# First layer: the adjacency loaded by converting transfers behind x, the first queries computed among the values, the mask stored later, and the queries' halves copied on SyncE's queue

## The reference

```python
h = relu(layernorm(x))
q, k, v = heads(h @ Wq.T + bq), heads(h @ Wk.T + bk), heads(h @ Wv.T + bv)    # 4 heads of 64
kc, vc = k and v cut into 8 chunks of 256 nodes
scores = clip(q @ kc.T / 8, -10, 10)                 # for each chunk
scores = where(mask == 0, -10, scores)               # mask = adj
ctx = sum over chunks of softmax(scores within the chunk) @ vc
out = layernorm(ctx @ Wo.T + bo + h) * gamma + beta
x = x + out
# second layer: additive attention over all 2048 nodes, masked by adj, softmax, elu; then x = x + that
```

## Time and profile before

| | us |
|---|---|
| median of 3 runs | 4921.1 |
| lowest, highest | 4913.72, 4924.88 |
| the profiled execution: time | 4913.24 |
| the profiled execution: span of the trace | 4911.4 |
| busy: PE, DVE, ACT, POOL | 4741.8, 3719.8, 2978.2, 1423.7 |
| first score product of batch 0 starts at | 105.11 |
| second layer's first instructions at | 3438.18 |

### The profile page before, as it was taken

One profiled execution on the slowest core, in us unless ns is written; L12 is line 12 of the kernel. 1 busy time (PEld: TensorE's weight loads), 2 busy tenths in 40 slices (PEclk: granted clock), 3 DMA queues, 4 the chain that ended last, 5 costly groups with the idle time before them and its releaser, 6 DMA issues. The chain is left out here.

```text
span 4911.4 us, 135734 instructions
## 1 busy us (share of the span) xinstructions
PE 4741.8 (97%) x56349; PEld 4357.3 (89%) x56349; DVE 3719.8 (76%) x7056; ACT 2978.2 (61%) x3317; POOL 1423.7 (29%) x1685
## 2 busy tenths in 40 slices
PE   6999999999999999999999999998899999999999
PEld 4998899898899988989988998987799999999998
DVE  6676666676676766666676676666899999999999
ACT  4444444444444444444444444443899999999998
POOL 3344334344334434434433443333100100000000
PEclk9999999999999999999999999999899999999999
DMA  6000100001000001001001000010421221221221
GB/s 214 18 18 18 30 19 27 23 18 27 19 23 27 18 23 27 18 19 31 18 18 32 18 27 18 17 40 12 114 73 36 76 74 35 76 78 31 76 65 37
DMA packets 173923, 195.25 MB, mean 40 GB/s; under 512 B 7520, under 2 KB 157408, under 8 KB 171104
## 3 DMA queue, kind: packets, MB, share of 16 engines
q1 hardware_dynamic: 158256, 142.70, 9.7%
q0 software_dynamic: 15024, 43.53, 3.6%
HBM read 110.43 MB, written 38.03 MB: 30 GB/s over the span
## 5 line engine op out<-in xcount | busy, mean ns | idle before, releaser
L797 ACT ACTIVATE slot<-slot,shift 128x1024 f32<-128x1024 f32 x1024 | 1113.6, 1088 | 1588.1 <-PE slot L651 1588.1
L661 PEld LDWEIGHTS outs<-v_s,probs 128*128 128x128 f32 x16384 | 1980.9, 192 | 103.5 <-issue 25.4
L661 PE MATMUL outs<-v_s,probs 128*128 128x128 f32 x16384 | 1991.6, 275 | 0.0
L941 DVE SCALAR_TENSOR_TENSOR probs<-slot,bound 128x1024 f32<-128x1024 f32 x1024 | 1253.2, 1224 | 681.2 <-ACT slot L797 678.3
L1577 ACT ACTIVATE u<-s_all,d_sign 128x1024 bf16<-128x1024 f32 x1024 | 1117.6, 1139 | 58.0 <-PE sums L1478 38.6
L459 POOL TENSOR_TENSOR ctx_sum<-ctx_sum,ctx_part 128x256 f32<-128x256 f32 x896 | 651.2, 732 | 1043.0 <-DVE ctx_part L957 1042.6
L650 PE MATMUL slot<-q_hl,k_hl 128*128 128x512 f32 x2048 | 897.4, 438 | 28.4 <-DVE probs L941 11.4
L651 PE MATMUL slot<-q_hl,k_hl 128*128 128x512 f32 x2048 | 805.0, 393 | 0.0
L1474 PE MATMUL sums<-x_mixed,u 128*128 128x130 f16 x8192 | 786.1, 219 | 2.0 <-issue 1.9
L1478 PE MATMUL sums<-x_mixed,mask 128*128 128x65 f16 x8192 | 759.5, 194 | 5.5 <-issue 5.5
L1709 DVE TENSOR_TENSOR u<-u,mask 128x1024 f16<-128x1024 bf16 x1024 | 688.1, 682 | 77.7 <-ACT u L1577 69.6
(11 more groups left out here) (161 smaller groups left out, 3766.6 us busy)
## 6 DMA issues: line engine op xcount, KB each, us to landing
q_hl<-q_hl POOLq DMA_DIRECT2D x128, 256.0 KB, 3.6
s_all<-s_turned SPq DMA_DIRECT2D x64, 512.0 KB, 5.5
x_q_s<-in_x SPq DMA_DIRECT2D x32, 512.0 KB, 4.8
x<-y SPq DMA_DIRECT2D x32, 512.0 KB, 3.2
t_o_s<-x SPq DMA_DIRECT2D x16, 1024.0 KB, 6.0
out<-t_o_s SPq DMA_DIRECT2D x16, 1024.0 KB, 6.8
x_q_s<-x SPq DMA_DIRECT2D x28, 512.0 KB, 6.1
probs<-in_adj SPq DMA_DIRECT2D x11, 1024.0 KB, 5.6
```

Source lines behind the costliest of these rows:

```text
L661: end = nc.tensor.matmul(outs[i % OUTS][:, q, :], probs[:, i % PROBS, r, q * P:(q + 1) * P], v_s[:, c * JC + r, h * E1:h * E1 + P], start= ...
L797: nc.scalar.activation(slot[:, :, :], slot[:, :, :], ACT.Exp, bias=shift[:, 0:1], scale=SCALE).then_inc(act_done, 1)
L941: nc.vector.scalar_tensor_tensor(probs[:, i % PROBS, :, :], spot(kind, "step", s, i)[:, :, :], P_LOW, bound[:, (i // H) % 2, :, :], ALU.ma ...
```

## The change

The loads of `adj` move from SP's queue to POOL's and convert int32 to fp16 on the way, into a ring of six places that lie in `probs` and `bound`; DVE's conversion (L846) is gone, and ACT writes the mask with the function Sign where it had Copy. SP begins with x. POOL issues tiles 0 and 1 behind the weights, tiles 2 to 5 ahead of 1/std, tiles 6 and 7 behind it and tile 8 + k behind the k-th residual; a load from tile 6 on waits until the tile six before it has been transposed. DVE no longer waits for the constants before it clears `v_s`. The first queries stand behind values 3 and 5 in the prologue too. The mask's store stands behind the store of strip 0. The queries' copies are issued by SP in all batches, without the small POOL instruction.

```diff
-ADJ_RING = 3
+ADJ_RING = 6
...
-        adj_in = [probs[:, 0:2, :, :].rearrange("p k r n -> p (k r n)").bitcast(I32),
-                  probs[:, 2:4, :, :].rearrange("p k r n -> p (k r n)").bitcast(I32),
-                  bound[:, :, :, :].rearrange("p k r n -> p (k r n)").bitcast(I32)]
-        adj16 = [ctx_part[:, :, :, :].rearrange("p h q d -> p (h q d)").bitcast(F16),
-                 ctx_sum[:, :, :, :].rearrange("p q h d -> p (q h d)").bitcast(F16)]
+        adj16 = [probs[:, k, :, :].rearrange("p r n -> p (r n)").bitcast(F16) for k in range(PROBS)]
+        adj16 += [bound[:, k, :, :].rearrange("p r n -> p (r n)").bitcast(F16) for k in range(2)]
...
-            load_adj(0)
-            load_adj(1)
             for s in range(NS):
                 load_strip(0, s)
-            for m in range(2, NT):
-                load_adj(m)
-            sp.wait_ge(mask_written, ADJ_PARTS * NT)
-            sp.dma_start(mask_dram, mask8[:, :, :]).then_inc(mask_stored, 16)
+
+            def copy_queries(qu, use):
+
+                sp.wait_ge(slot_free, use + 1 + SLOTS)
+                for r in range(2):
+                    own, other = slice(r * D, (r + 1) * D), slice((1 - r) * D, (2 - r) * D)
+                    sp.dma_start(q_hl[other, 2 * qu + r, :, :].bitcast(F32), q_hl[own, 2 * qu + r, :, :].bitcast(F32))\
+                        .then_inc(q_copied[qu], 16)
+
+            for qu in range(Q_USES):
+                copy_queries(qu, q_first(qu))
...
                 for s in range(NS - 1):
+                    for qu in range(Q_USES):
+                        copy_queries(qu, used(b, kind, "q", s + 1, qu))
...
                     store(b, s)
+                    if first and s == 0:
+                        sp.dma_start(mask_dram, mask8[:, :, :]).then_inc(mask_stored, 16)
...
+                if not last:
+                    for qu in range(Q_USES):
+                        copy_queries(qu, used(b, kind, "q", 0, qu))
...
+            def load_adj(m):
+
+                if m >= ADJ_RING:
+                    pool.wait_ge(adj_transposed, ADJ_PARTS * (m - ADJ_RING + 1))
+                pool.dma_start(adj16[m % ADJ_RING], adj[m * P:(m + 1) * P, :]).then_inc(adj_loaded[m % ADJ_RING], 16)
+
             for dst, src in consts:
                 pool.dma_start(dst, src).then_inc(consts_loaded, 16)
+            load_adj(0)
+            load_adj(1)
...
+            for m in range(2, ADJ_RING):
+                load_adj(m)
             inverse_std(1, slice(0, NT))
+            load_adj(ADJ_RING)
+            load_adj(ADJ_RING + 1)
             pool.wait_ge(consts_loaded, 16 * len(consts))
             for k in range(T_USES):
                 pool.wait_ge(slot_filled, t_first(k) + 1)
                 residual(k + 1, hs[:, 2 * k:2 * k + 2, :])
-            for qu in range(Q_USES):
-                copy_queries(qu, q_first(qu))
+                load_adj(ADJ_RING + 2 + k)
...
             def mask_tile(m):
-                pe.wait_ge(adj_cast, m + 1)
+                pe.wait_ge(adj_loaded[m % ADJ_RING], (m // ADJ_RING + 1) * 16)
...
-            for qu in range(Q_USES):
-                queries(0, qu, q_first(qu), slots[q_first(qu) % SLOTS])
+                if k in Q_AFTER_V:
+                    qu = Q_AFTER_V.index(k)
+                    queries(0, qu, q_first(qu), slots[q_first(qu) % SLOTS])
...
-                                         ACT.Copy).then_inc(mask_written, 1)
+                                         ACT.Sign).then_inc(mask_written, 1)
...
-            dve.wait_ge(consts_ready, 4)
             dve.sem_inc(x1_stored, 1)
...
-            def mask_tile(m):
-                dve.wait_ge(adj_loaded[m % ADJ_RING], (m // ADJ_RING + 1) * 16)
-                if m >= 2:
-                    dve.wait_ge(adj_transposed, ADJ_PARTS * (m - 1))
-                nc.vector.tensor_scalar(adj16[m % 2], adj_in[m % ADJ_RING], 0.0, None, ALU.is_gt).then_inc(adj_cast, 1)
```

More of the change, by code:

```diff
@@ L288, in v_first @@
         def v_first(k):
[L289 removed]
+            return T_USES + K_USES + k + sum(at < k for at in Q_AFTER_V)
         def q_first(qu):
[L292 removed]
+            return T_USES + K_USES + Q_AFTER_V[qu] + qu + 1
         def used(b, kind, *name):
@@ L460, in add @@
                                         ALU.add).then_inc(ctx_added, 1)
-            def copy_queries(qu, use):
-                pool.wait_ge(slot_free, use + 1 + SLOTS)
-                nc.gpsimd.tensor_tensor(query_cell[:, qu:qu + 1], pool_cell[:, 1:2], pool_cell[:, 1:2], ALU.add)
-                for r in range(2):
-                    own, other = slice(r * D, (r + 1) * D), slice((1 - r) * D, (2 - r) * D)
-                    pool.dma_start(q_hl[other, 2 * qu + r, :, :], q_hl[own, 2 * qu + r, :, :]).then_inc(q_copied[qu], 16)
             def finish(b, s, first, end):
@@ L526, in batch @@
                                          hs[:, (s - 1) * IT + 2 * pair:(s - 1) * IT + 2 * pair + 2, :])
-                if not last:
-                    for qu in range(Q_USES):
-                        copy_queries(qu, used(b, kind, "q", 0, qu))
+            for m in range(2, ADJ_RING):
+                load_adj(m)
             inverse_std(1, slice(0, NT))
+            load_adj(ADJ_RING)
+            load_adj(ADJ_RING + 1)
             pool.wait_ge(consts_loaded, 16 * len(consts))
@@ L557, in mask_tile @@
                         jt = part * per + t
-                        last = nc.tensor.transpose(adj_t[part][:, t, :], adj16[m % 2][:, jt * P:(jt + 1) * P], ident16)
+                        last = nc.tensor.transpose(adj_t[part][:, t, :], adj16[m % ADJ_RING][:, jt * P:(jt + 1) * P], ident16)
                     last.then_inc(adj_transposed, 1)
```

26 lines of the change are left out of this document (4 added, 22 removed).

## The result

The changed kernel took 4886.16 us (median of 4 executions, 4879.97 to 4886.92) where the kernel before took 4919.16 us (4913.72 to 4924.88) beside it: ratio 0.9932, 95% interval 0.9921 to 0.9944. The forecast was 4900 us, 13.8 us too high, and the result stands at the low end of its range. The profiled execution took 4885.47 us with a span of 4883.7 us: 27.8 us of span are gone, where the forecast had 21.

The account below looks back on a forecast made before the run. PE, busy 97% of the span, was taken as the bound, so only its waits and lower clock could be won. Terms 6.1 + 0.8 + 2.4 + 1.0 + 8.0 + 0.7 + 2.0 = 21 us gave a 4900 us median, range 4886 to 4919.

Parts of the forecast that it names:

- x first: Prologue's start: without two adj tiles ahead of it, x lands at 14.0 us instead of 20.14; 6.1 us won.
- 1/std: Prologue, POOL: the addition falls from 1.10 to 0.3 us without DVE's conversion beside it, the power stays 3.81; 0.8 us won.
- Transposes: Prologue, transposes of h: same instructions in the same order, 0 us; keys reach ACT at 40.6 us.
- Keys and converting loads: Prologue, eight key uses with mask tiles: 3.35 us each, 2.4 us won; converting loads keep up at 3.4 us a tile.
- both rivals on late loads: Prologue: adj loads take over 3.9 us a tile (chance 0.13), or 6.9 by the read side, giving 4948 us (0.07).
- The equal share for x: Prologue rival: POOL's queue shares bandwidth equally, x lands at 15.7 us; 3 us less gain, 4903; no separate chance given.
- Queries: Prologue's end: with queries among the values, PE's 8.02 us wait for their copies ahead of batch 0 goes; 8.0 us won.
- The mask's store: Moved beside strip 1: the 4 MB end well before the loads that follow are used, so the move costs nothing.
- Clock and second pair: Batch 0, first score to first values product: 4.2 us instead of 4.96, with 1.1 to 1.8 us of wait; 0.7 won.
- Copies in the batches: All batches, queries' copies issued by SP instead of POOL: 2 us won, at least 0 and at most 3.1.
- Within these bounds the copy is hidden: Batches: at 2.8 to 9.5 us a copy, median 3.6, and 4.6 from issue to use, PE does not wait.
- Copies from SP land later: Batches, rival: at 5.6 us to landing, 31 strip starts lose 1.0 us each, giving 4933 us; chance 0.04.

Follow-up runs that it names:

- e5: Kernel before with x loaded first on SP's queue, conversions and plain adj loads kept: 4916.59 us, ratio 0.9994.
- f2: Kernel before with x loaded first, conversions kept, and DVE's wait for the constants ahead of clearing v_s removed: 4916.75 us, ratio 0.9995.
- e10: Changed kernel with DVE's wait for POOL's constants ahead of clearing v_s put back: 4885.60 us, ratio 0.9935.
- e9: Kernel before with the first queries behind values 3 and 5 and the mask's store behind the store of strip 0: 4909.27 us, ratio 0.9982.
- e2: Changed kernel with the last batch's 2 MB load of x1 issued between the two query pairs' copies: 4894.22 us, ratio 0.9954.
- e6: Changed kernel with the mask's 4 MB store put back ahead of the first queries' copies: 4885.98 us, ratio 0.9937.

## Why the prediction was right and wrong

- **x first, 6.1 us.** Place and size were right: 13.93 us for 14.0. That it stands alone was wrong (e5: 0.35 us, f2: 2.9 us). The clearing "while x is on its way, as before" hung on a deleted wait that the forecast had not priced (e10).
- **1/std, 0.8 us.** It was 0.88 for the addition and 0.87 more for the power, 2.94 for 3.81 us. By the Trainium skill (SBUF — State Buffer, "Who interferes with whom") a DVE instruction in a two-port mode and a GpSimd one shut each other out. The trace agrees for the addition: 1.10 us in the earlier trace rows and in f2 with a conversion beside it, 0.22 without.
- **Transposes, 0.** The normalization took 9.48 us instead of 7.45, which brought the keys to 41.28 instead of 40.6 us. PE waited 5.49 us for DVE, up to 34.1 us, and its granted clock was 0.50 from 31.1 to 37.9 us, where in the kernel before the same transposes ran at 1.00. What that stretch cost by itself is not shown.
- **Keys and converting loads.** 3.37 us an iteration for 3.35; no transpose behind the first waited for a load. From 16 to 34 us, below, the engines moved 208 to 218 GB/s by bytes written, so 0.52 MB in 2.4 to 2.5 us for the 3.4 assumed and the 3.9 allowed, and both rivals on late loads fell. The estimate from the Trainium skill (DMA: Bandwidth & Descriptors, "Anatomy of one DMA") was 2.4 us. The equal share for x, at 15.7 us, did not come.

DMA view of the changed kernel from 0 to 90 us, 40 slices of 2.25 us each; the converting loads run alone in the eighth to the fifteenth:

```profile
GB/s 12 300 356 364 343 262 179 213 217 211 211 215 217 208 218 198 11 127 113 53 180 146 127 188 113 144 173 115 171 0 0 0 0 7 0 4 36 197 0 213
```

- **Queries, 8.0 us.** The size was right (e9: 8.37), the cause was half of it. Early queries give 0.44 us; the step that failed is *"The mask's store: 4 MB, now beside strip 1. ... Nothing."* It looked at what the store does in its new place and not at what it did in the old. That front and queries together came to 18.2 us for the forecast's 18.3 is in part luck: its terms were off both ways, and the other executions with this prologue had 16.2 to 17.5.
- **Clock and second pair, 0.7 us won.** It was 2.2 us lost in the traced execution: from first score to first values product 5.54 us for 4.2. The wait was 2.34 us for 1.1 to 1.8, and the clock fell.
- **Copies in the batches, 2 us.** The places that this term covers gave 11.5 us in the traces, and this is the step behind most of the error: *"Within these bounds the copy is hidden."* Hidden it is at 23 strip starts inside the batches and at the starts of batches 2 to 6, not at the starts of batches 1 and 7, nor at the last strip of batch 7, where 2 MB went first (7.3 us). The 4 waits, 11.1 us, of the earlier trace rows were taken for all there was, though waits for copies were booked on DVE's clip or on "issue" too: 2.17 us at batch 1 and 3.70 at the last strip. And "at most 3.1" priced waits alone, not the half clock behind them: 6.8 us of it at the last strip, 3.4 at each of two batch starts. One of these two, 1.8 us at batch 6, stood behind a wait that the clip ended: it belongs to the clock, which is partly chance, and not to a late copy. The forecast also asked what is queued behind the copies on SP and not which transfer they now precede. "Copies from SP land later" fell: 3.7 us.

Sum in the traces: front and queries 18.2, lost behind them 2.2, batch starts 4.2, last strip of batch 7 7.3, small steps 0.4: 27.9 for 21. The 5 us beyond that in the medians may be the batch starts, where the kernel before's profiled execution had 2 half-clock stretches for a mean of 3.1; that accounts for 2 us, and with an interval of 6 us to either side the rest is within the scatter.

## What to carry to other kernels

A small transfer that the bounding engine waits for must be issued ahead of every large one, whatever queue each is on; where a change moves a queue's work, list the large transfers that it passes, and price also what a moved transfer did in its old place. A wait shown on a compute engine that had long been done can be a DMA's: look up its landing before calling it hidden, and at each kind of start apart. Split a semaphore when two transfers share it and the consumer needs the first one sooner (1.3 us of wait in batch 0 here, though the whole gain stayed within the scatter).

## What the runs showed of the hardware that was not expected

- A 256 KB copy within SBUF, issued from either queue, lands in a median of 3.6 to 3.7 us, but in up to 9.5 us behind a 2 MB load and 11.6 us behind a 4 MB store and a 0.5 MB load, all on another queue, and in up to 9.7 and 10.0 us behind the same load and the same store on its own queue (e2, e6).
- By bytes read the converting loads of int32 went at 416 to 436 GB/s, twice the written side, where the earlier trace rows gives 304 written and 152 read for uint8, over a window in which the DMA engines were busy for 74.7%. So neither side alone gives one rate for both. That the larger side sets it would fit, but is not shown. In a row the loads landed 2.4 to 2.5 us apart; one by itself (from the tenth on) took 5.1 to 5.3 us from issue to landing.
- DVE's normalization pieces take 0.40 us alone, 0.69 beside POOL's maximum with 0 (L458), 1.43 beside its addition (L460), and one took 1.57 us from the end of a load's issue into that maximum; beside the issues alone they took 0.40 to 0.56. Which pieces meet them moved the sixteen from 7.44 us (f2) to 9.48 us. Groups of the changed kernel and of the kernel before, with the mean of one in ns:

```profile
L855 DVE TENSOR_SCALAR h_q_s<-x_q_s,moments,rstd 128x256 f32<-128x256 f32 x16 | 9.5, 666 | 3.4 <-POOL rstd L453 3.4
```

```profile
L862 DVE TENSOR_SCALAR h_q_s<-x_q_s,moments,rstd 128x256 f32<-128x256 f32 x16 | 7.4, 543 | 2.9 <-POOL rstd L442 2.9
```

- The granted clock fell from 2.4 to 1.2 GHz for 3.4 us behind 24 of the 91 counted waits at batch starts, of 1.83 to 3.01 us, and stayed up behind others of up to 2.29 us (f2, batch 1) and behind 2.31 us in batch 0 of e10: part chance, and 1.6 to 3.4 us each time, the wait included.
